# A graph kernel's block product moved to the third step, and its gathers tied to other events of TensorE

## The reference

```python
msg_b = jnp.einsum('ei,bio->ebo', h[src], weight)
msg = jnp.einsum('ebo,eb->eo', msg_b, w_comp[etype]) * edge_weight[:, None]
x1 = layernorm(x + relu(segment_sum(msg, dst) + bias))
norm = edge_weight / segment_sum(edge_weight, dst)[dst]     # 0 where the sum is 0
x2 = layernorm(x1 + segment_sum(norm[:, None] * (x1 @ W)[src], dst) + b)
```

## Time and profile before

| | |
|---|---|
| median of three runs | 2789.37 us (2783.76 to 2796.03) |
| profiled execution | 2792.45 us, span 2790.6 us |
| mean granted TensorE clock | 0.787 |
| busy, share of the span | PE 66%, PEld 49%, DVE 46%, ACT 30%, POOL 53% |
| bytes moved, all queues | 299.95 MB, 107 GB/s over the span |

### The profile page before, as it was taken

How to read it: one execution, slowest core, us unless ns; L and a number is a source line. 1 busy time by engine, 2 the same in 40 slices (tenths; PEclk the granted TensorE clock), 3 DMA queues, 4 the chain that set the end, 5 groups by cost and what they waited for, 6 DMA issues and landing times.

```text
span 2790.6 us, 61390 instructions
## 1 busy us (share of the span) xinstructions
PE 1847.3 (66%) x21470; PEld 1358.6 (49%) x21470; DVE 1293.7 (46%) x3623; ACT 850.7 (30%) x2171; POOL 1491.9 (53%) x1590
## 2 busy tenths in 40 slices
PE   3565655656566666666767767666667776677786
PEld 2343434434344444454545555455555555555654
DVE  5454443544445444454444454444544434444446
ACT  3333322323233332233322333232333223223212
POOL 4555555555555555555555555555555554555430
PEclk8777676776677778787787788888888887888897
DMA  4233333323232343333333333333234333333466
GB/s 96 69 109 108 110 106 108 98 71 100 95 100 76 110 123 111 118 89 116 100 103 86 107 107 100 110 118 117 63 102 129 99 115 81 96 104 107 124 215 204
DMA packets 197571, 299.95 MB, mean 107 GB/s; under 512 B 66502, under 2 KB 137083, under 8 KB 191135
## 3 DMA queue, kind: packets, MB, share of 16 engines
q1 hardware_dynamic: 99496, 167.96, 17.1%
q0 software_dynamic: 50112, 51.41, 9.4%
q10 hardware_dynamic: 47671, 76.76, 9.2%
HBM read 187.43 MB, written 108.56 MB: 106 GB/s over the span
## 4 chain that ended last, share of the span: by engine, by line
PE 50%; another core or an unknown queue 19%; issue 16%; ACT 7%; ACTq 4%; DVE 3%; DMA 1%; DVEq 0%; SPq 0%
PE coefs_ps L1362 6%; PE node_ps L1272 6%; PE coefs_ps L1396 6%; PE sums_ps L1272 6%; ACT room L1069 5%; PE types_ps L1272 5%; PE dense_ps L1272 4%; PE sums_ps L1309 4%; PE sums_ps L1296 3%; PE node_ps L1282 2%; ACTq L649 2%; PE coefs_ps L1257 1%; PE sums_ps L1282 1%; PE types_ps L1282 1%
## 5 line engine op out<-in xcount | busy, mean ns | idle before, releaser
L837 POOL DMA_INDIRECT gathered_rows<-in_x,idx x1559 | 1472.0, 944 | 1212.0 <-issue 396.5
L1932 DVE TENSOR_TENSOR dve_ps<-coefs_ps,edges 128x32 f32<-128x32 f32 x196 | 38.7, 198 | 947.6 <-remote 542.9
L1069 ACT COPY room<-dense_ps 128x294 f32 x390 | 168.7, 433 | 714.9 <-PE dense_ps L1272 256.1
L1910 DVE TENSOR_TENSOR first_room<-first_room,dve_ps 128x1024 bf16<-128x1024 bf16 x585 | 364.7, 677 | 0.0
L1282 PE MATMUL node_ps<-carry_hot,first_room 128*128 128x49 bf16 x1170 | 109.0, 202 | 313.0 <-ACT room L1069 252.2
L1272 PE MATMUL sums_ps<-first_room 128*128 128x245 bf16 (+1 forms) x1170 | 267.3, 339 | 52.3 <-issue 52.0
L1282 PEld LDWEIGHTS node_ps<-carry_hot,first_room 128*128 128x128 bf16 x1170 | 84.9, 109 | 384.6 <-ACT room L1069 302.2
L1272 PE MATMUL dense_ps<-first_room 128*128 128x245 bf16 x1170 | 240.1, 317 | 41.7 <-issue 36.3
L1069 ACT COPY room<-node_ps 128x294 f32 x390 | 168.3, 432 | 318.1 <-remote 157.0
L1396 PE MATMUL coefs_ps<-acc_room,x_nodes 128*64 128x107 f32 x2742 | 229.3, 297 | 51.2 <-issue 50.8
L1272 PE MATMUL types_ps<-first_room 128*128 128x245 bf16 x1170 | 247.4, 328 | 12.0 <-issue 11.4
(11 more groups left out here) (300 smaller groups left out, 2598.5 us busy)
## 6 DMA issues: line engine op xcount, KB each, us to landing
acc_room<-block_table ACTq DMA_DIRECT2D x147, 374.5 KB
block_table<-room SPq DMA_DIRECT2D x11, 2621.5 KB
type_rows<-in_edge_type SPq DMA_DIRECT2D x260, 96.0 KB
gathered_rows<-in_x,idx POOLq DMA_INDIRECT x1559
block_table<-room SPq DMA_DIRECT2D x9, 2247.0 KB
block_table<-room SPq DMA_DIRECT2D x9, 1872.5 KB
block_table<-room SPq DMA_DIRECT2D x10, 1498.0 KB
acc_room<-block_table ACTq DMA_DIRECT2D x43, 321.0 KB
```

The costliest lines, as they stand in the source:

```text
L837: pool.indirect_dma_start(gathered_rows[:, s, j, 0:D], None, rows, bass.IndirectOffsetOnAxis(ap=idx[:, s, j:j + 1], axis=0)).then_inc(rows ...
L1069: nc.scalar.copy(blocks_out[:, h % 2, :, bass.ds(offset, nodes)], dense_ps[j % 4][:, 0:nodes * TILES].rearrange("p (w h) -> p h w", h=TILE ...
L1910: last = nc.vector.tensor_tensor(lo_hot[:, w, q0:q1, :, :], lo_hot[:, 2, q0:q1, :, :], part_of_weights(w), ALU.mult)
```

## The change

The product of block i - 1 moves from the second step to the third, in the same place within the step. The taking of the partial moves by a step too: VectorE takes it while TensorE is in the first step of the next iteration, and there TensorE waits for it, ahead of visits and look-up. SP's program is the same, so its store of the partial waits for the later event.

POOL's four waits per group become, for the group gathered in TensorE's third step (s = 0): 1 chunk, 5 chunks, 8 chunks, the product. In its first step (s = 1): 1 chunk, 3 chunks, the placing of parts, 8 chunks. In its second step (s = 2): 1 chunk, 4 chunks, the placing, 8 chunks. No wait is on the look-up.

```diff
-GATHERED_BEHIND = {0: 3, 2: 6, 4: 8}
-BEHIND_COEFS = 6
+GATHERED_BEHIND = ({0: 1, 2: 5, 4: 8}, {0: 1, 2: 3, 6: 8}, {0: 1, 2: 4, 6: 8})
+BEHIND_PLACES = (None, 4, 4)
+BEHIND_BLOCK = (6, None, None)
@@ gather_group
-                    if behind_dense and j in GATHERED_BEHIND:
-                        pool.wait_ge(dense_summed, step * CH + (FREE_HOTS - CH + GATHERED_BEHIND[j]))
+                    if behind_dense and j in GATHERED_BEHIND[s]:
+                        pool.wait_ge(dense_summed, step * CH + (FREE_HOTS - CH + GATHERED_BEHIND[s][j]))
                         pool.sem_inc(gathers_paced, 1)
-                    if behind_dense and j == BEHIND_COEFS:
-                        pool.wait_ge(coefs_ready, step)
+                    if behind_dense and j == BEHIND_PLACES[s]:
+                        pool.wait_ge(group_summed, step + (FREE - 2))
+                        pool.sem_inc(gathers_paced, 1)
+                    if behind_dense and j == BEHIND_BLOCK[s]:
+                        pool.wait_ge(block_applied, of_iter - 1)
                         pool.sem_inc(gathers_paced, 1)
@@ TensorE, between (mixed steps)
-                        if s == 2 and tiles_done(i - 1):
-                            pe.wait_ge(partial_taken, i)
+                        if s == 0 and tiles_done(i - 2):
+                            pe.wait_ge(partial_taken, i - 1)
@@ TensorE, the step of the main loop
                         use_coefs(step)
+                        if s == 0 and tiles_done(i - 2):
+                            pe.wait_ge(partial_taken, i - 1)
                         if s == 2 and tiles_done(i - 1):
-                            pe.wait_ge(partial_taken, i)
-                        if s == 1 and tiles_done(i - 1):
                             apply_block(i - 1, i - 1)
@@ VectorE, take_of
-                    if step % U == 1 and tiles_done(step // U - 1):
+                    if step % U == 2 and tiles_done(step // U - 1):
                         take_partial(step // U - 1, step // U - 1)
```

More of the change, by code:

```diff
@@ L205 @@
 assert sum(FETCHED_ROWS) == P and len(FETCHED) <= 32 and FETCHED[-1] < ITERS - 1
-assert 2 * FETCHES > FIRST_REGULAR + 1 and max(GATHERED_BEHIND.values()) <= CH
+assert 2 * FETCHES > FIRST_REGULAR + 1 and max(max(found.values()) for found in GATHERED_BEHIND) <= 2 * CH
 assert 0 < TAIL <= CH and FIRST_TILE[-1] == TILES and GROUPS <= 2 * P
@@ L814, in _, with gather_group @@
                            allow_small_or_imprecise_dtypes=True).then_inc(consts_ready, 1)
-            def gather_group(step, s, chunks, rows, behind_dense=False, behind_sums=False):
+            def gather_group(step, s, chunks, rows, behind_dense=False, behind_sums=False, of_iter=None):
                 pool.wait_ge(idx_ready, step + 1)
@@ L851, in gather_iter @@
                     for s in range(U):
-                        gather_group(m * (FETCHES * U) + (v * U + s), s, chunks[s], x[:, :], behind_dense, not behind_dense)
+                        gather_group(m * (FETCHES * U) + (v * U + s), s, chunks[s], x[:, :], behind_dense, not behind_dense, m * FETCHES + v)
                 whole, but_one = (CH, CH, CH), (CH, CH, CH - 1)
@@ L863, in _ @@
                     for s in range(U):
-                        gather_group(i * U + s, s, CH, x[:, :], True)
+                        gather_group(i * U + s, s, CH, x[:, :], True, False, i + 0)
                 gather_group(ITERS * U, 0, TAIL, x[:, :])
```

## The result

The changed kernel takes 2828.95 us (median of four runs, 2824.99 to 2841.08), the kernel before, run beside it, 2786.57 (median of four, 2780.55 to 2796.03): a ratio of 1.0161, 95% interval 1.0138 to 1.0185. It is slower by 42 us. The forecast was 2750; the time lies in its range and inside the band of the slower rival.

What follows compares the result with a forecast made beforehand. POOL waits on late signals from TensorE, which POOL's own runs of gathers hold up: 1868.5 us of gathers plus 815.5 of waits. Terms -64 + 21 + 0 + 0 + 3 = -40 us gave 2750, range 2725 to 2775.

Steps and rivals of the forecast that it cites:

- First, the wait on the look-up goes: POOL's fourth pairs: 36 look-up waits fall from 3.7 to 1.9 us each, -64 us, between 0 and -132.
- Second, the first pair waits for its indices: First pair of a group: one more wait for indices in every second iteration, +21 us, between 0 and +85.
- Third, the run across the end of the third step is cut: Third step's end: six gathers in a row become four and two; between +87 and -130 us, taken as 0.
- Fourth, the product in the third step: TensorE's second step loses the product, the third gains it: 0; ScalarE's later clearing +73 us if uncovered, taken as 0.
- Fifth, the queues: Loop's end: late visits' loads and the block's store queue closer to their use, 0 to +10 us, +3 taken.
- The clock: TensorE's granted clock: 0.08 more bought nothing, so 0; as a rival, second step slower, 2816 us, chance 0.02.
- The rule weighed: Skill's rule on TensorE's clock: long idle gaps slow it, so a second step without product runs slower; held not borne out.
- Longer runs and a late clearing: Slower rival: pairs join into runs of six and ScalarE clears before the parts' copy, 2819 to 2840 us; chance 0.25.
- The shorter hold decides: Rival: the cut run at the third step's end gives TensorE 2.5 us in most iterations, 2616 to 2681 us; chance 0.13.
- Nothing to win: Rival: in late iterations POOL's look-up wait is a result, its time returns as index waits, 2789 us; chance 0.20.
- signs that I had called right: POOL's look-up group gone, its 815.5 us of waits about 775; ScalarE's idle before the parts' copy from 6 to about 4.
- the signs called wrong: POOL's waits not falling, idle before ScalarE's clearing, TensorE's room waits beyond 2.54 us, or last look-up to late visit over 5 longer.

Runs made afterwards that it cites:

- the kernel with the look-up kept: Changed kernel, but in the first and second step the fourth pair waits for the look-up again, not the eighth chunk: 2797.84 us, ratio 1.0035.
- the product alone: Changed kernel with the old waits for all three groups, the product left in the third step: 2790.53 us, ratio 1.0017.
- the last pair free: Product in the third step and old waits, but the fourth pair of the first and second step at the eighth chunk: 2821.85 us, ratio 1.0272.
- four gathers behind the look-up: Product in the third step; pairs at three and six chunks, then four gathers together behind the look-up: 2822.5 us, ratio 1.0257.

## Why the prediction was wrong

The time before plus the parts as the runs give them (ratios against the kernel before, from two sets and the result, in which the kernel before took 2787 to 2792 us; each has an interval of 0.002 either way, so a difference is good to some 0.003): the product's place +0.0017, the third step's last pair behind the product -0.0046, the spacing of the other pairs +0.0064 (from 0.9971 to the 1.0035 of the kernel with the look-up kept), the look-up wait dropped in two steps +0.0126 (from 1.0035 to 1.0161). In us: +5, -13, +18, +35, together +45, which is the ratio's 1.0161; the medians give 42. That they add up is no check, as each term starts where the last one ends, and in another order the terms would differ: the waits without the product's move cost 125.

- *"First, the wait on the look-up goes", -64.* This is the step that failed: +35 us with the new spacing, 31 to 70 with the old, where the bounds were 0 and -132. It is 99 us off, of 85 between the forecast's -40 and +45; the other terms together are 14 off the other way. The term lets each of 36 waits fall to the 1.9 us of an ordinary restart, as if the pair kept a stop of its own. The reading of the rows was right, POOL did stand 132 us there, and so was the mechanism that the same text gives (TensorE is held by POOL's runs). But the term was priced on POOL's side alone, by what a wait costs the engine that waits. It left out what the wait did for the others: it ended a run. Without it 47 runs reach eight instead of 26 and 831 gathers lie in runs of six or more instead of 900, so what grew is the longest runs. That the wait costs time when it is dropped is shown; that it does so through the joined runs rests on these counts, the stretch above, and the second kind of chip, where there is no hold and dropping it changes nothing (1.0027 against 1.003). The upper bound "0, the same time is waited for at the next pair" leaves a loss out without a reason; the third part, where both sides were priced, had one.
- *"Second, the first pair waits for its indices", +21.* The waits for indices fell from 130.9 us in 45 to 96.0 in 30, and the old first wait gave nothing back (1.0184). The term as told is not there. The +18 us for the whole of the new spacing happens to have its size, by something else.
- *"Third, the run across the end of the third step is cut", 0 between -130 and +87.* Measured -13 us, between two chips: within its ends, and on the side of the shorter hold.
- *"Fourth, the product in the third step", 0.* Right with the old waits, 1.0017; with the new ones the move and the last pair behind it together give some 80 us back, which the prediction didn't have. ScalarE's clearing got idle time in front of it, 89 us in the changed kernel and 145 with the product alone, where the time shows no cost. In 22 of the 30 times that the changed kernel's clearing had more than 0.5 us of it, the copy behind it stood for 0.6 us or more after the clearing.
- *"Fifth, the queues", +3.* Nothing to be seen. The timelines of the loop's end in the changed kernel:

```profile
2727.40 0.27 DVE L2148 COPY partials<-coefs_ps 128x107 f32<-128x107 f32 x1
...
2728.12 2.74 SPq L650 DMA_DIRECT2D room<-block_table  x6
...
2734.78 1.25 PE L1423 MATMUL dense_ps<-room,x_nodes 128*64 128x321 f32 x8
```

  From the partial to the first late visit are 7.4 us where the earlier trace rows have 17.0. The loads are issued closer to their use, and TensorE starts on them at once. From the first late visit to the end of the span are 88 us, before 90, so the loss is all within the loop.
- *The clock, 0.* The kernel with the look-up kept and the changed one have the granted clocks 0.776 and 0.778 and TensorE busy for 1895.8 and 1888.7 us, and are 31 us apart, so the clock doesn't account for what the dropped look-up wait costs. The spacing may: from one pair behind the product to the look-up kernel the clock falls from 0.791 to 0.776 and TensorE is busy 54 us more, for +18 us. The rule weighed was that long idle gaps bring the slower level back (the Trainium skill, TensorE: Matmul & The Clock Gate, "Why this matters for your kernels"). The two ends fit it, 0.791 in the fastest kernel of this kind of chip with all its gathers and 0.745 in the slowest; whether the clock is cause or result there, and what share of the time it makes, was not measured.

Of the rivals, "Longer runs and a late clearing" had the sign and the time (2819 to 2840 us). Its first half is what happened: pairs found their events over and joined. Its number was right by luck: its +73 was the clearing, which cost nothing that shows in the time, and the -64 in it was none either. Its ground, that every wait in the earlier trace rows is at a floor of 2 us, isn't so in the rows themselves: one is 0.65. "The shorter hold decides" was true of one pair in twelve and small. "Nothing to win" took the last pair's waits for a result of TensorE's own time; taking them away would then be free, and it wasn't.

Of what was to show it: the look-up's group went and the sum of waits fell as said (to 789.6, "about 775"), both signs that I had called right, while the time rose. They were the wrong signs to watch. The idle time ahead of the parts' copy fell too. Of the signs called wrong one came, the clearing with idle time in front. TensorE's waits for `room` didn't grow (252.2 to 134.3 us in the largest group, the longest 8.0 to 4.5), nor did the time from the last whole look-up to the first late visit (8.4 us in both). ScalarE's "remote" at the chunks doesn't rank the kernels either: it is 762.2 us in the changed kernel, but 686.6 in the look-up kernel, which loses almost nothing, and 539.8 with the last pair free, which loses as much. What grew in most of the slower kernels is POOL's longest wait for a chunk: 4.7 us before, 5.1 to 6.0 in the three within 0.4% of it, 8.6 to 13.3 in the slower ones, except with four gathers behind the look-up (3.7).

## What to carry to other kernels

A wait that costs its engine time may break up a burst that hurts others; before taking it out, ask what the instructions behind it join up with, and price the burst on the engines beside it. Bound a removed wait from both sides, a loss too, and count run lengths in the trace, not only the sum of the waits. Measure the kernel before on every chip that a variant runs on: here the same edits were worth up to 6.6% on one kind and under 0.5% on the other.

## What was not expected of the hardware

The kernel before took 2788.57, 2744.31, 2788.46, 2791.77 and 2751.01 us in five sets and 2048.23 and 2047.59 in two. The kernel with one pair behind the product on a chip of the second kind, first its page, then waits of POOL and TensorE:

```profile
PE 1499.1 (73%) x21470; PEld 1190.5 (58%) x21470; DVE 1289.2 (63%) x3623; ACT 862.2 (42%) x2171; POOL 1498.0 (73%) x1590
...
PE 33%; POOL 28%; issue 15%; DMA 9%; DVE 6%; ACTq 3%; SPq 2%; ACT 2%; DVEq 1%; POOLq 1%
...
L845 POOL DMA_INDIRECT gathered_rows<-in_x,idx x1559 | 1478.1, 948 | 477.8 <-issue 416.8
```

```profile
POOL gathered_rows L845 <- issue: 416.8, 1367, 0.4
POOL gathered_rows L845 <- PE sums_ps L1280: 19.2, 63, 0.3
POOL gathered_rows L845 <- ACT idx L951: 7.0, 15, 2.8
...
PE sums_ps L1304 <- DMA gathered_rows<-in_x,idx: 302.9, 89, 9.7
```

A gather takes 948 ns on either, and VectorE and ScalarE are as busy as on the other kind (1294.8 and 855.5 us for the same kernel). But a wait of POOL costs 0.3 us where it cost 2.3, no release is unnamed in the chain, 1542 of the 1559 gathers lie in runs of six or more without harm, and POOL itself is near the bound: 1559 x 1.25 = 1949 of 2052 us. TensorE is granted 0.876 and is 343 us less busy. It also hardly stops without a named reason: its idle time under "issue" is 84 us in 31 gaps, and 529 us in 671 for the same kernel on the first kind. So the hold during gathers in a row, on which the whole case turns, belongs to some chips and not to others. The same kernel takes 2782.66 - 2053.41 = 729 us more there, and POOL waits 807 us, its idle time without "issue", where it waits 61. How much of that is late signals, how much TensorE's own stops and how much the clock isn't separated. What makes the difference between the chips the runs don't show. On the second kind all variants with all their gathers cost 0.3 to 0.5% (the interval of the last pair free reaches 1), also with only one pair moved; as each of them has the product in the third step, that is the likely cause, argued and not shown. The changed kernel itself did not run there.
